# Cross-attention and feed-forward kernel: first loads on two queues, fewer warm-up matmuls, wq centred head by head on two engines

## The chip, the cores and the metric

The kernel runs on one core of a Trainium2 chip (trn2). The metric is the device time in microseconds of one execution. The kernel before took 117.61 us, the median of three runs (117.22, 117.66 and 117.61).

## The reference

```python
def xattn(x, context, Wq, Wk, Wv, Wo, bo):      # 8 heads of 128
    q = (x @ Wq).reshape(B, Tq, h, C) * SCALE    # SCALE = 128 ** -0.25
    k = (context @ Wk).reshape(B, Tk, h, C) * SCALE
    v = (context @ Wv).reshape(B, Tk, h, C)
    attn = softmax(einsum('bqhc,bkhc->bhqk', q, k))
    out = einsum('bhqk,bkhc->bqhc', attn, v).reshape(B, Tq, h * C)
    return out @ Wo + bo

x = x + xattn(layernorm(x), ctx_768, Wq, Wk, Wv, Wo, bo)
x = x + ffn(layernorm(x), Ws1, Ws2, W1, W2, Wr)
```

x is 2 x 1024 x 256, the context 2 x 77 x 192, all in fp32. The ffn is a shared expert, square(relu(x @ Ws1)) @ Ws2, and eight routed ones. Each routed one is multiplied by a truncated softmax weight of the two best logits, which is zero unless the gap between them is large. The kernel computes the largest gap and branches to the routed part only if it needs it.

## The kernel before

The kernel folds the weights first. For each head, A = (centred Wq) x (scaled K) turns the scores into x times A, so that q is never formed; in the same way U = V x Wo turns the output into probabilities times U. The mean over the 256 inputs of each column of Wq is taken off (the centring), which stands in for the mean in layernorm. A and U are split into a high and a low fp32r part (`a_hi`, `a_lo`), and so is x transposed (`xt_hi`, `xt_lo`), so that each product is three fp32r matmuls (the helper `three`, L433 to L437). After this opening come 16 tiles of 128 rows of x, each with scores, softmax, attention and feed-forward. They are software-pipelined over tiles, in a loop of two tiles a turn.

The order of work on each engine is written out by hand, with one block for each engine and semaphores between them. The part that this document is about is the opening:

- SyncE issues all the loads on its own DMA queue: ctx, the two main parts of wk, the second part of ctx, the tail of wk, four pieces of wq_t (two heads each), then x transposed, x, ws1 and wr, wv, wo, bo, ws2 and the rest of x (L336 to L364).
- TensorE runs WARM_UP = 9 matmuls on a constant (L566), each of which the trace shows as two records. Then it computes K from ctx and wk: `context_main` (L405, 8 matmuls, 16 records) and `context_tails` (L415), which need the two parts of ctx and all of wk. Then `make_a` (L429), two matmuls a head, in the order of the heads. Then the scores of tile 0, first half (`alo_ready` at least 4), a small matmul for the mean of the ffn weights (L580), the second half of the scores (all 8 of `a_lo`), and the scores of tile 1.
- VectorE sums each head of wq as it lands and scales the sum to minus the mean (`mean_of_wq`, L1074 and L1076): head 0, head 1, then three pairs. Each of the ten steps adds one to `wqs`. Then it makes the eight `a_lo` (`lo_of_a`, L1081), the centred ffn weights (L1091), and the statistics of x.
- ScalarE copies and scales K out of PSUM, two heads at a time (L741, `kt_copied`), centres heads 0, 4 and 5 (`centre_wq`, L737), and makes the eight `a_hi` (L749). Its exponentials of tile 0 follow.
- GpSimd centres heads 1, 2 and 3, 6 and 7 (L862), then splits x transposed of tiles 0 and 1 (`turned_x`, L817 and L822).

The first four banks of A are the ones that K is computed in, so `make_a` also waits for `kt_copied` of h + 1 for its first four heads, which counts pairs. The centring waits read so:

```python
if h in (0, 4, 5):
    pe.wait_ge(wqact_ready, (1, 2, 3)[(0, 4, 5).index(h)])
else:
    pe.wait_ge(wqpool_ready, {1: 1, 2: 2, 3: 2, 6: 3, 7: 3}[h])
if h < H // 2:
    pe.wait_ge(kt_copied, h + 1)
```

Of the kernel before, what the change touches and what calls it, by code (L numbers as in the profile page):

```python
# [34 lines left out]
P = 128  # L35
# [8 lines left out]
def program(nc, x, x_t, ctx_p, wq_t, wk_p, wv_p, wo, bo, ws1, ws2, w1, w2, wr, out):  # L44
    B, TQ, D = x.shape
# [15 lines left out]
    assert B == 2 and FE == P and TILES % 4 == 0 and HALF <= 512 and KC == 5 and DCH == 2  # L61
    GATE_STEPS = 5
    OPEN_FROM = 272.0
    WARM_UP = 9
    HALFP = P // 2
    assert WB == HG + 2 and HG == 4
    PB = (KC - 1) * P
# [5 lines left out]
    with ExitStack() as ctx:  # L73
# [243 lines left out]
        def wait_apart(eng, semaphore, count):  # L317
# [2 lines left out]
            eng.wait_ge(const_ready, 4)  # L320
            eng.wait_ge(semaphore, count)

        block = ctx.enter_context(nc.Block())


        @block.sync
        def _(sp):
            wq_rows = wq_t.rearrange("(h p) d -> p h d", p=P)

            def load_wq(i):  # L330
                sp.dma_start(wqt_sb[:, 2 * i:2 * i + 2, :], wq_rows[:, 2 * i:2 * i + 2, :]).then_inc(wq_in[i], 16)

            def load_wv(i):
                sp.dma_start(wv_sb[:, i, :, :].rearrange("p e c -> p (e c)"), wv_p[:, i, :]).then_inc(wv_in[i], 16)

            sp.dma_start(ctx_sb[:, 0, :], ctx_p[:, 0, :]).then_inc(ctx_in, 16)  # L336
            for i in range(2):
                sp.dma_start(wk_sb[:, i, 0:HG, :].rearrange("p e c -> p (e c)"), wk_p[:, i, 0:HG * P]).then_inc(wk_in[i], 16)
            sp.dma_start(ctx_sb[:, 1, :], ctx_p[:, 1, :]).then_inc(ctx_tail_in, 16)
            sp.dma_start(wk_sb[:, :, HG:WB, :].rearrange("p i e c -> p i (e c)"), wk_p[:, :, HG * P:WB * P]).then_inc(wk_tail_in, 16)  # L340
            for i in range(4):
                load_wq(i)

            def load_x_t(i):
                for c in range(DCH):
# [53 lines left out]
        def _(pe):  # L399
# [19 lines left out]

            def make_a():  # L420
                for h in range(H):
                    if h in (0, 4, 5):
                        pe.wait_ge(wqact_ready, (1, 2, 3)[(0, 4, 5).index(h)])
                    else:
                        pe.wait_ge(wqpool_ready, {1: 1, 2: 2, 3: 2, 6: 3, 7: 3}[h])
                    if h < H // 2:
                        pe.wait_ge(kt_copied, h + 1)
                    for c in range(DCH):
                        mm = pe.matmul(a_banks[h][:, c * BK:(c + 1) * BK], wqt_sb[:, h, c * P:(c + 1) * P],  # L429
                                       kt_sb[:, h, :], start=True, stop=True)  # L430
                    mm.then_inc(a_ready, 1)
# [246 lines left out]
        def _(act):  # L678
# [56 lines left out]
            def centre_wq(h, count):  # L735
                act.wait_ge(wqs, count)
                act.activation(wqt_sb[:, h, :], wqt_sb[:, h, :], ACT.Identity, bias=wq_mean[:, 1, h:h + 1]).then_inc(wqact_ready, 1)  # L737

            for g in range(H // 2):
                act.wait_ge(kt_ready, g + 1)  # L740
                act.activation(kt_sb[:, 2 * g:2 * g + 2, :].rearrange("p h n -> p (h n)"), s_ps[:, g, 0:2 * BK],  # L741
                               ACT.Copy, scale=SCALE2).then_inc(kt_copied, 1)
                if g == 0:
                    centre_wq(0, 2)
            centre_wq(4, 8)
            centre_wq(5, 8)
            for h in range(H):
                act.wait_ge(a_ready, h + 1)
                act.activation(a_hi[:, :, :, h * TK:(h + 1) * TK],  # L749
                               a_banks[h][:, 0:DCH * BK].rearrange("p (c b k) -> p c b k", c=DCH, b=B),  # L750
                               ACT.Copy).then_inc(ahi_ready, 1)
            exps(0, 0, 0)
            exps(0, 0, 1)
            for g in range(H // 2):
# [52 lines left out]
        def _(pool):  # L807
# [38 lines left out]
            def step(t, par):  # L846
                normalise(t, par, 0)
                if live(t + 2, TILES):
# [7 lines left out]
            pool.wait_ge(const_ready, 3)  # L856
            pool.affine_select(out=ident[:, :], in_=ident[:, :], compare_op=ALU.not_equal, fill=1.0, base=0,
                               pattern=[[-1, P]], channel_multiplier=1).then_inc(const_ready, 1)
            for first, heads, count in ((1, 1, 4), (2, 2, 6), (6, 2, 10)):
                hs = slice(first, first + heads)  # L860
                pool.wait_ge(wqs, count)
                pool.tensor_tensor(wqt_sb[:, hs, :], wqt_sb[:, hs, :],  # L862
                                   wq_mean[:, 1, hs].unsqueeze(2).broadcast_to([P, heads, D]), ALU.add).then_inc(wqpool_ready, 1)
            turned_x(0, 0)
            turned_x(1, 1)
            rstd_first(0)
# [45 lines left out]
        def _(dve):  # L912
# [141 lines left out]
            def all_stats_x(t, par):  # L1054
                stats_x(t, par)
                dve.wait_ge(bn1_done, t + 1)
                aggregate_x(t, par)
                variance_x(t, par)
# [19 lines left out]
            def lo_of_a(h):  # L1078
                dve.wait_ge(ahi_ready, h + 1)
                at = (slice(None), slice(None), slice(None), slice(h * TK, (h + 1) * TK))  # L1080
                dve.tensor_tensor(a_lo[at], a_banks[h][:, 0:DCH * BK].rearrange("p (c b k) -> p c b k", c=DCH, b=B),  # L1081
                                  a_hi[at].bitcast(F32), ALU.subtract).then_inc(alo_ready, 1)
# [4 lines left out]
                mean_of_wq(i, 2 * i, 2, 2 * i + 3)  # L1087
            for h in range(H):
                lo_of_a(h)
            dve.wait_ge(wmean_ready, 1)  # L1090
            dve.tensor_tensor(wsr_c[:, :, :], wsr_sb[:, :, :],  # L1091
                              wmean_bank[:, 0:NL].unsqueeze(1).broadcast_to([P, DCH, NL]), ALU.subtract).then_inc(wsr_ready, 1)
            dve.wait_ge(x_in[0], 32)
            all_stats_x(0, 0)
            maxima(0, 0)
            neg_maxima(0, 0)
            all_stats_x(1, 1)
# [163 lines left out]
```

## Time and profile before

| | us |
|---|---|
| runs | 117.22, 117.66, 117.61 |
| profiled execution, its own time | 117.36 |
| its span, first to last instruction | 115.5 |
| TensorE matmul busy | 109.2 (95%) |
| VectorE busy | 87.8 (76%) |
| ScalarE busy | 85.5 (74%) |
| GpSimd busy | 65.5 (57%) |

Mean granted clock of TensorE is 0.993 of full speed. The span is cut into stretches by the windows view; the chain view follows the work that ended last back from the last instruction; the timeline gives each group of instructions with its start and duration. PE is TensorE, DVE VectorE, ACT ScalarE, POOL GpSimd, SPq and ACTq the DMA-issuing queues of SyncE and ScalarE. L737 is line 737 of the kernel.

### The profile page before, as it was taken

How to read it: one execution, taken by the hardware profiler on the slowest of the kernel's cores; microseconds unless marked ns; L12 is line 12 of the kernel's file. 1: busy time of each engine (PE TensorE's matmuls, PEld its weight loads, DVE VectorE, ACT ScalarE, POOL GpSimd, SP SyncE). 2: the span in 40 equal slices, each digit the busy share in tenths (PEclk: the TensorE clock that was granted, in tenths of full speed). 3: DMA queues.
4: the chain of work that ended last, by engine and by line, in shares of the span. 5: the costliest groups of instructions: out<-in, count | busy, mean ns of one | idle time of the engine just before them, and what ended most of it. 6: DMA issues, size and time to landing. Idle time of an engine off the chain costs nothing.

```text
span 115.5 us, 3118 instructions
## 1 busy us (share of the span) xinstructions
PE 109.2 (95%) x854; PEld 105.9 (92%) x854; DVE 87.8 (76%) x350; ACT 85.5 (74%) x348; POOL 65.5 (57%) x106
## 2 busy tenths in 40 slices
PE   6976999999999999999999999999999999989981
PEld 6974999899998989999999999999999999979970
DVE  1009888569889697797979797797979696798963
ACT  4006925997948979898988889898988889994320
POOL 2005735855372965785676578657746865469250
PEclk9999999999999999999999999999999999999997
DMA  3799999994000200040005001300500050031032
GB/s 63 252 336 357 354 355 350 346 349 160 6 6 0 91 0 3 6 146 35 0 0 182 0 0 61 121 0 0 182 0 0 0 182 3 0 124 57 38 136 98
DMA packets 11815, 12.70 MB, mean 110 GB/s; under 512 B 1056, under 2 KB 10272, under 8 KB 11808
## 3 DMA queue, kind: packets, MB, share of 16 engines
q1 hardware_dynamic: 11520, 12.36, 32.4%
q10 hardware_dynamic: 288, 0.26, 0.7%
q8 instruction: 3, 0.05, 0.2%
q14 instruction: 4, 0.03, 0.1%
HBM read 8.42 MB, written 2.10 MB: 91 GB/s over the span
## 4 chain that ended last, share of the span: by engine, by line
PE 80%; DVE 7%; DMA 4%; ACT 2%; SPq 2%; issue 2%; POOL 1%; DVEq 0%; ACTq 0%
PE o_ps L435 8%; PE o_ps L437 8%; PE o_ps L436 8%; PE s_ps L435 7%; PE s_ps L437 7%; PE s_ps L436 7%; PE g_ps L493 6%; PE f_ps L523 4%; DMA wqt_sb<-in_wq_t 4%; PE g_ps L506 3%; PE f_ps L435 2%; PE g_ps L449 2%; ACT probs L712 1%; PE f_ps L437 1%; PE f_ps L436 1%
## 5 line engine op out<-in xcount | busy, mean ns | idle before, releaser
L712 ACT ACTIVATE probs<-s_ps,neg_max,rstd 128x77 f32<-128x77 f32 x112 | 45.2, 425 | 4.0 <-DVE neg_max L950 4.0
L840 POOL TENSOR_TENSOR probs<-probs,recip 128x308 f32<-128x308 f32 x27 | 18.9, 701 | 23.4 <-DVE recip L956 23.3
L712 ACT ACTIVATION_READ_ACCUMULATOR probs<-s_ps,neg_max,rstd 128x1 f32 x112 | 24.0, 214 | 0.0
L435 PE MATMUL o_ps<-u_hi,pt_hi 128*128 128x256 f32 (+1 forms) x80 | 22.7, 284 | 0.5 <-DVE pt_lo L964 0.5
L437 PE MATMUL o_ps<-u_lo,pt_hi 128*128 128x256 f32 (+1 forms) x80 | 22.4, 280 | 0.0
L436 PE MATMUL o_ps<-u_hi,pt_lo 128*128 128x256 f32 (+1 forms) x80 | 22.4, 280 | 0.0
L435 PE MATMUL s_ps<-a_hi,xt_hi 128*128 128x308 f32 x64 | 22.1, 345 | 0.0
L437 PE MATMUL s_ps<-a_lo,xt_hi 128*128 128x308 f32 x64 | 19.5, 304 | 0.0
L436 PE MATMUL s_ps<-a_hi,xt_lo 128*128 128x308 f32 x64 | 19.4, 303 | 0.0
L435 PEld LDWEIGHTS o_ps<-u_hi,pt_hi 128*128 128x128 f32 (+1 forms) x80 | 15.0, 188 | 0.9 <-DVE pt_lo L964 0.9
L436 PEld LDWEIGHTS o_ps<-u_hi,pt_lo 128*128 128x128 f32 (+1 forms) x80 | 15.1, 188 | 0.0
L437 PEld LDWEIGHTS o_ps<-u_lo,pt_hi 128*128 128x128 f32 (+1 forms) x80 | 15.0, 188 | 0.0
L942 DVE TENSOR_REDUCE row_max<-s_ps 128x8 f32<-128x616 f32 x16 | 12.4, 775 | 2.1 <-PE s_ps L437 2.1
L983 DVE TENSOR_TENSOR x_tr<-o_ps,xb_sb 128x256 f32<-128x256 f32 x14 | 5.9, 424 | 9.7 <-PE o_ps L437 9.7
L822 POOL TENSOR_TENSOR xt_lo<-xt_sb,xt_hi 128x256 fp32r<-128x256 f32 x16 | 11.7, 728 | 2.2 <-POOL xt_hi L820 0.2
L435 PEld LDWEIGHTS s_ps<-a_hi,xt_hi 128*128 128x128 f32 x64 | 12.1, 188 | 0.2 <-issue 0.2
L436 PEld LDWEIGHTS s_ps<-a_hi,xt_lo 128*128 128x128 f32 x64 | 12.1, 190 | 0.0
L437 PEld LDWEIGHTS s_ps<-a_lo,xt_hi 128*128 128x128 f32 x64 | 12.0, 188 | 0.0
L844 POOL TENSOR_TENSOR xb_sb<-x_sb,bo_sb 128x256 f32<-128x256 f32 x16 | 11.7, 737 | 0.0
L493 PE MATMUL g_ps<-ident,probs 128*128 128x128 f32 x66 | 10.1, 273 | 0.0
L968 DVE TENSOR_TENSOR pt_lo<-g_ps,pt_hi 128x512 fp32r<-128x512 f32 x13 | 8.9, 687 | 1.1 <-ACT pt_hi L698 0.6
L698 ACT ACTIVATE pt_hi<-g_ps 128x512 fp32r<-128x512 f32 x13 | 7.8, 601 | 1.7 <-PE g_ps L493 1.7
(188 smaller groups left out, 270.6 us busy)
## 6 DMA issues: line engine op xcount, KB each, us to landing
xt_sb<-in_x_t SPq DMA_DIRECT2D x8, 256.0 KB, 6.4
x_sb<-in_x SPq DMA_DIRECT2D x8, 256.0 KB, 6.3
x_sb<-x_tr SPq DMA_DIRECT2D x7, 256.0 KB, 2.3
out<-y_sb SPq DMA_DIRECT2D x6, 256.0 KB, 2.3
wqt_sb<-in_wq_t SPq DMA_DIRECT2D x4, 256.0 KB, 5.2
wo_sb<-in_wo SPq DMA_DIRECT2D x1, 1024.0 KB, 8.9
wk_sb<-in_wk_p SPq DMA_DIRECT2D x3, 256.0 KB, 3.2
wv_sb<-in_wv_p SPq DMA_DIRECT2D x2, 384.0 KB, 6.2
```

The lines of the kernel that those rows point to most:

```text
L435: pe.matmul(out_ap, hi, rhs_hi, start=first, stop=False)
L436: pe.matmul(out_ap, lo, rhs_hi, start=False, stop=False)
L437: return pe.matmul(out_ap, hi, rhs_lo, start=False, stop=last)
L493: mm = pe.transpose(to, probs_of(t)[:, par, c * P:(c + 1) * P], ident[:, :])
L698: act.activation(pt_hi[:, 0:PB], main_turned(t), ACT.Copy).then_inc(pthi_ready, 1)
L712: e = act.activation(probs_of(t)[:, par, h * TK:(h + 1) * TK], s_ps[:, 2 * par + half, (h - half * H // 2) * TK:(h - half * H // 2 + 1) * TK],
L822: pool.tensor_tensor(xt_lo[:, par, :, :], src, xt_hi[:, par, :, :].bitcast(F32), ALU.subtract).then_inc(xt_ready, 1)
L840: pool.tensor_tensor(rows, rows, recip[:, par, hs].unsqueeze(2).broadcast_to([P, H // 2, TK]), ALU.mult).then_inc(probs_ready, 1)
L844: pool.tensor_tensor(xb_sb[:, par, :], x_sb[:, t, :], bo_sb[:, :], ALU.add).then_inc(xb_ready, 1)
L942: dve.tensor_reduce(row_max[:, par, :].rearrange("p (i h) -> p i h", i=2), s_ps[:, 2 * par:2 * par + 2, 0:HALF].rearrange("p i (h k) -> p ...
L968: dve.tensor_tensor(pt_lo[:, 0:PB], main_turned(t), pt_hi[:, 0:PB].bitcast(F32), ALU.subtract).then_inc(ptlo_ready, 1)
L983: dve.tensor_tensor(x1_of(t, par), o_ps[:, 0:D], xb_sb[:, par, :], ALU.add).then_inc(x1_ready, 1)
```

## The change

WARM_UP goes from 9 to 6. Of the first nine loads, ScalarE now issues ctx part 0, wk main 1, ctx part 1, wq pieces 0 and 2, ahead of all its other work; SyncE issues wk main 0, the wk tail, wq pieces 1 and 3, and then goes on as before. ScalarE centres heads 0, 2, 4 and 6, GpSimd heads 1, 3, 5 and 7, each head by itself, and ScalarE's copies of K, centrings and `a_hi` are interleaved in a new order. VectorE takes the statistics of x of tile 0 before the centred ffn weights instead of after them.

```diff
--- before.py
+++ after.py
@@ -61,7 +61,7 @@
     assert B == 2 and FE == P and TILES % 4 == 0 and HALF <= 512 and KC == 5 and DCH == 2
     GATE_STEPS = 5
     OPEN_FROM = 272.0
-    WARM_UP = 9
+    WARM_UP = 6
     HALFP = P // 2
     assert WB == HG + 2 and HG == 4
     PB = (KC - 1) * P
@@ -320,26 +320,26 @@
             eng.wait_ge(const_ready, 4)
             eng.wait_ge(semaphore, count)
 
+        wq_rows = wq_t.rearrange("(h p) d -> p h d", p=P)
+
+        def load_wk(eng, i):
+            eng.dma_start(wk_sb[:, i, 0:HG, :].rearrange("p e c -> p (e c)"), wk_p[:, i, 0:HG * P]).then_inc(wk_in[i], 16)
+
+        def load_wq(eng, i):
+            eng.dma_start(wqt_sb[:, 2 * i:2 * i + 2, :], wq_rows[:, 2 * i:2 * i + 2, :]).then_inc(wq_in[i], 16)
+
         block = ctx.enter_context(nc.Block())
 
 
         @block.sync
         def _(sp):
-            wq_rows = wq_t.rearrange("(h p) d -> p h d", p=P)
-
-            def load_wq(i):
-                sp.dma_start(wqt_sb[:, 2 * i:2 * i + 2, :], wq_rows[:, 2 * i:2 * i + 2, :]).then_inc(wq_in[i], 16)
-
             def load_wv(i):
                 sp.dma_start(wv_sb[:, i, :, :].rearrange("p e c -> p (e c)"), wv_p[:, i, :]).then_inc(wv_in[i], 16)
 
-            sp.dma_start(ctx_sb[:, 0, :], ctx_p[:, 0, :]).then_inc(ctx_in, 16)
-            for i in range(2):
-                sp.dma_start(wk_sb[:, i, 0:HG, :].rearrange("p e c -> p (e c)"), wk_p[:, i, 0:HG * P]).then_inc(wk_in[i], 16)
-            sp.dma_start(ctx_sb[:, 1, :], ctx_p[:, 1, :]).then_inc(ctx_tail_in, 16)
+            load_wk(sp, 0)
             sp.dma_start(wk_sb[:, :, HG:WB, :].rearrange("p i e c -> p i (e c)"), wk_p[:, :, HG * P:WB * P]).then_inc(wk_tail_in, 16)
-            for i in range(4):
-                load_wq(i)
+            load_wq(sp, 1)
+            load_wq(sp, 3)
 
             def load_x_t(i):
                 for c in range(DCH):
@@ -419,10 +419,10 @@
 
             def make_a():
                 for h in range(H):
-                    if h in (0, 4, 5):
-                        pe.wait_ge(wqact_ready, (1, 2, 3)[(0, 4, 5).index(h)])
+                    if h % 2 == 0:
+                        pe.wait_ge(wqact_ready, h // 2 + 1)
                     else:
-                        pe.wait_ge(wqpool_ready, {1: 1, 2: 2, 3: 2, 6: 3, 7: 3}[h])
+                        pe.wait_ge(wqpool_ready, h // 2 + 1)
                     if h < H // 2:
                         pe.wait_ge(kt_copied, h + 1)
                     for c in range(DCH):
@@ -736,19 +736,35 @@
                 act.wait_ge(wqs, count)
                 act.activation(wqt_sb[:, h, :], wqt_sb[:, h, :], ACT.Identity, bias=wq_mean[:, 1, h:h + 1]).then_inc(wqact_ready, 1)
 
-            for g in range(H // 2):
+            act.dma_start(ctx_sb[:, 0, :], ctx_p[:, 0, :]).then_inc(ctx_in, 16)
+            load_wk(act, 1)
+            act.dma_start(ctx_sb[:, 1, :], ctx_p[:, 1, :]).then_inc(ctx_tail_in, 16)
+            load_wq(act, 0)
+            load_wq(act, 2)
+
+            def kt_pair(g):
                 act.wait_ge(kt_ready, g + 1)
                 act.activation(kt_sb[:, 2 * g:2 * g + 2, :].rearrange("p h n -> p (h n)"), s_ps[:, g, 0:2 * BK],
                                ACT.Copy, scale=SCALE2).then_inc(kt_copied, 1)
-                if g == 0:
-                    centre_wq(0, 2)
-            centre_wq(4, 8)
-            centre_wq(5, 8)
-            for h in range(H):
+
+            def hi_of_a(h):
                 act.wait_ge(a_ready, h + 1)
                 act.activation(a_hi[:, :, :, h * TK:(h + 1) * TK],
                                a_banks[h][:, 0:DCH * BK].rearrange("p (c b k) -> p c b k", c=DCH, b=B),
                                ACT.Copy).then_inc(ahi_ready, 1)
+
+            kt_pair(0)
+            centre_wq(0, 2)
+            kt_pair(1)
+            centre_wq(2, 6)
+            kt_pair(2)
+            kt_pair(3)
+            centre_wq(4, 8)
+            hi_of_a(0)
+            hi_of_a(1)
+            centre_wq(6, 10)
+            for h in range(2, H):
+                hi_of_a(h)
             exps(0, 0, 0)
             exps(0, 0, 1)
             for g in range(H // 2):
@@ -856,11 +872,10 @@
             pool.wait_ge(const_ready, 3)
             pool.affine_select(out=ident[:, :], in_=ident[:, :], compare_op=ALU.not_equal, fill=1.0, base=0,
                                pattern=[[-1, P]], channel_multiplier=1).then_inc(const_ready, 1)
-            for first, heads, count in ((1, 1, 4), (2, 2, 6), (6, 2, 10)):
-                hs = slice(first, first + heads)
+            for h, count in ((1, 4), (3, 6), (5, 8), (7, 10)):
                 pool.wait_ge(wqs, count)
-                pool.tensor_tensor(wqt_sb[:, hs, :], wqt_sb[:, hs, :],
-                                   wq_mean[:, 1, hs].unsqueeze(2).broadcast_to([P, heads, D]), ALU.add).then_inc(wqpool_ready, 1)
+                pool.tensor_tensor(wqt_sb[:, h:h + 1, :], wqt_sb[:, h:h + 1, :],
+                                   wq_mean[:, 1, h:h + 1].unsqueeze(2).broadcast_to([P, 1, D]), ALU.add).then_inc(wqpool_ready, 1)
             turned_x(0, 0)
             turned_x(1, 1)
             rstd_first(0)
@@ -1087,11 +1102,11 @@
                 mean_of_wq(i, 2 * i, 2, 2 * i + 3)
             for h in range(H):
                 lo_of_a(h)
+            dve.wait_ge(x_in[0], 32)
+            all_stats_x(0, 0)
             dve.wait_ge(wmean_ready, 1)
             dve.tensor_tensor(wsr_c[:, :, :], wsr_sb[:, :, :],
                               wmean_bank[:, 0:NL].unsqueeze(1).broadcast_to([P, DCH, NL]), ALU.subtract).then_inc(wsr_ready, 1)
-            dve.wait_ge(x_in[0], 32)
-            all_stats_x(0, 0)
             maxima(0, 0)
             neg_maxima(0, 0)
             all_stats_x(1, 1)
```

SyncE, from its first load to its last piece of wq. Before:

```order
L336 DMA ctx_sb<-in_ctx_p 128x154
L338 DMA wk_sb<-in_wk_p 128x512 x2
L339 DMA ctx_sb<-in_ctx_p 128x154
L340 DMA wk_sb<-in_wk_p 128x2x256
L331 DMA wqt_sb<-in_wq_t 128x2x256 x4
L346 DMA xt_sb<-in_x_t 128x2x256 x2
```

and with the change:

```order
L326 DMA wk_sb<-in_wk_p 128x512
L340 DMA wk_sb<-in_wk_p 128x2x256
L329 DMA wqt_sb<-in_wq_t 128x2x256 x2
L346 DMA xt_sb<-in_x_t 128x2x256 x2
L351 DMA x_sb<-in_x 128x2x256 x2
```

Of nine loads four are left on this queue (the ctx and half of the wk and wq pieces have gone), and `xt_sb`, x transposed, stands right behind its two pieces of wq.

ScalarE, from its first instruction to the last `a_hi` (`wqt_sb` is wq, head by head). Before:

```order
L741 ACT_TABLE_LOAD
L741 ACTIVATE kt_sb<-s_ps 128x308
L737 ACTIVATE wqt_sb<-wqt_sb,wq_mean 128x256
L741 ACTIVATE kt_sb<-s_ps 128x308 x3
L737 ACTIVATE wqt_sb<-wqt_sb,wq_mean 128x256 x2
L749 ACTIVATE a_hi<-s_ps 128x4x77 x4
L749 ACTIVATE a_hi<-g_ps 128x4x77 x2
L749 ACTIVATE a_hi<-o_ps 128x4x77
L749 ACTIVATE a_hi<-f_ps 128x4x77
```

and with the change, up to the first of the later `a_hi`:

```order
L739 DMA ctx_sb<-in_ctx_p 128x154
L326 DMA wk_sb<-in_wk_p 128x512
L741 DMA ctx_sb<-in_ctx_p 128x154
L329 DMA wqt_sb<-in_wq_t 128x2x256 x2
L747 ACT_TABLE_LOAD
L747 ACTIVATE kt_sb<-s_ps 128x308
L737 ACTIVATE wqt_sb<-wqt_sb,wq_mean 128x256
L747 ACTIVATE kt_sb<-s_ps 128x308
L737 ACTIVATE wqt_sb<-wqt_sb,wq_mean 128x256
L747 ACTIVATE kt_sb<-s_ps 128x308 x2
L737 ACTIVATE wqt_sb<-wqt_sb,wq_mean 128x256
L752 ACTIVATE a_hi<-s_ps 128x4x77 x2
```

Five DMA issues stand ahead of the load of the activation table, the third and fourth copy of K (`kt_sb`) stand behind the centring of head 2, and the centring of head 6 stands between the second `a_hi` and the third.

VectorE, from the last `a_lo` to the first row maxima and their negation. Before:

```order
L1081 TENSOR_TENSOR a_lo<-f_ps,a_hi 128x4x77
L1091 TENSOR_TENSOR wsr_c<-wsr_sb,g_ps 128x272
L914 BN_STATS bn<-x_sb 128x6
L917 BN_AGGR mv<-bn 128x2
L921 TENSOR_SCALAR var<-mv 128x1
L942 TENSOR_REDUCE row_max<-s_ps 128x8
L950 TENSOR_SCALAR neg_max<-row_max,rstd 128x8
```

and with the change:

```order
L1096 TENSOR_TENSOR a_lo<-f_ps,a_hi 128x4x77
L929 BN_STATS bn<-x_sb 128x6
L932 BN_AGGR mv<-bn 128x2
L936 TENSOR_SCALAR var<-mv 128x1
L1108 TENSOR_TENSOR wsr_c<-wsr_sb,g_ps 128x272
L957 TENSOR_REDUCE row_max<-s_ps 128x8
L965 TENSOR_SCALAR neg_max<-row_max,rstd 128x8
```

The centred ffn weights (`wsr_c`) have moved from ahead of the statistics of x to behind them.

## Rows read from the trace of the kernel before

**Rows 1.** Windows: busy per engine in us, granted clock, DMA share, GB/s.

```profile
16.20:28.20 12.00, 12.00 (x97) 11.68 (x96) 9.25 (x30) 9.32 (x44) 6.73 (x12) 1.00 1.02 321
...
41.40:101.30 59.90, 59.90 (x483) 59.84 (x484) 49.52 (x215) 53.05 (x230) 38.47 (x60) 1.00 0.12 44
```

**Rows 2.** Chain of waits: start us, us, what.

```profile
3.30 5.07 DMA wqt_sb<-in_wq_t
...
10.39 1.05 POOL wqt_sb L862
...
11.48 1.32 PE s_ps L429 x8
```

**Rows 3.** Timeline of the SyncE queue: start us, us, DMA issue, count.

```profile
0.74 0.39 SPq L336 DMA_DIRECT2D ctx_sb<-in_ctx_p  x1
...
1.19 0.88 SPq L338 DMA_DIRECT2D wk_sb<-in_wk_p  x2
...
2.59 0.67 SPq L340 DMA_DIRECT2D wk_sb<-in_wk_p  x1
...
3.30 2.12 SPq L331 DMA_DIRECT2D wqt_sb<-in_wq_t  x4
```

**Rows 4.** DMA issues, in order of issue: count, KB each, us to landing.

```profile
wk_sb<-in_wk_p SPq DMA_DIRECT2D x1, 256.0 KB, 2.9
...
wk_sb<-in_wk_p SPq DMA_DIRECT2D x1, 256.0 KB, 5.0
...
wqt_sb<-in_wq_t SPq DMA_DIRECT2D x1, 256.0 KB, 5.1
...
xt_sb<-in_x_t SPq DMA_DIRECT2D x2, 256.0 KB, 5.5
```

**Rows 5.** Windows of the first 10 us, columns as in rows 1.

```profile
0.00:3.00 3.00, 1.94 (x9) 1.94 (x10) 0.29 (x4) 1.28 (x1) 0.78 (x8) 1.00 0.37 71
3.00:4.00 1.00, 1.00 (x7) 1.00 (x6) 0.00 (x0) 0.00 (x0) 0.00 (x0) 1.00 0.95 338
4.00:6.00 2.00, 2.00 (x15) 2.00 (x15) 0.00 (x0) 0.00 (x0) 0.00 (x0) 1.00 0.73 214
6.00:7.00 1.00, 1.00 (x10) 0.95 (x8) 0.00 (x0) 0.00 (x0) 0.00 (x0) 1.00 1.02 315
7.00:10.00 3.00, 1.91 (x21) 1.53 (x20) 1.54 (x5) 1.40 (x4) 0.41 (x1) 1.00 1.07 349
```

**Rows 6.** Timeline of TensorE: start us, us, operation, count, idle before.

```profile
1.06 4.02 PE L567 MATMUL f_ps<-mean_of 128*128 128x128 f32 x18 [1.06 <-DVE probs L1068]
...
4.92 2.26 PE L405 MATMUL s_ps<-ctx_sb,wk_sb 128*128 128x154 f32 x16
...
7.77 1.32 PE L415 MATMUL s_ps<-ctx_sb,wk_sb 64*128 64x154 f32 x16 [0.59 <-DMA wk_sb<-in_wk_p]
```

**Rows 7.** Timeline of ScalarE.

```profile
0.74 1.28 ACT L741 ACT_TABLE_LOAD   x1 [0.74 <-PEq L1255]
...
8.57 0.43 ACT L741 ACTIVATE kt_sb<-s_ps 128x308 f32<-128x308 f32 x1 [6.54 <-PE s_ps L415]
...
11.49 0.91 ACT L737 ACTIVATE wqt_sb<-wqt_sb,wq_mean 128x256 f32<-128x256 f32 x2 [1.00 <-DVE wq_mean L1076]
...
12.30 1.36 ACT L749 ACTIVATE a_hi<-s_ps 128x308 fp32r<-128x308 f32 x4
```

**Rows 8.** Timeline of VectorE.

```profile
12.07 0.17 DVE L1076 TENSOR_SCALAR wq_mean<-wq_mean 128x2 f32<-128x2 f32 x1
...
12.74 1.64 DVE L1081 TENSOR_TENSOR a_lo<-s_ps,a_hi 128x308 fp32r<-128x308 f32 x4 [0.50 <-ACT a_hi L749]
...
15.45 0.47 DVE L1081 TENSOR_TENSOR a_lo<-f_ps,a_hi 128x308 fp32r<-128x308 f32 x1
```

**Rows 9.** Timeline of GpSimd.

```profile
13.30 0.40 POOL L817 CAST xt_hi<-xt_sb 128x256 fp32r<-128x256 f32 x1
...
13.78 0.73 POOL L822 TENSOR_TENSOR xt_lo<-xt_sb,xt_hi 128x256 fp32r<-128x256 f32 x1
```

## Prediction

> **What bounds the kernel now.** I read three views in this order. The windows by stage come first. From 16.2 us on TensorE has no idle microsecond in the opening (12.00 of 12.00) nor in the loop (59.90 of 59.90) [rows 1]. No term of the sum is in that part, so an early microsecond moves the end only if TensorE gets to its steady work sooner. The chain of waits says what holds it back: the first piece of wq lands at 3.30 + 5.07 = 8.37, VectorE's sums follow, GpSimd centres heads 2 and 3 until 11.44, and from 11.48 on TensorE works without a hole [rows 2]. The timelines show a second path that is nearly as late: the tail of wk lands at 7.6 (issued 2.59, 5.0 to landing) [rows 3, 4], TensorE has waited 0.59 us for it [rows 6], and ScalarE's first copy of K starts at 8.57, that is 0.80 after those matmuls [rows 7]. The stretch of VectorE's eight `a_lo` ends at 15.45 + 0.47 = 15.92 [rows 8]. TensorE's second half of the scores of tile 0 needs the last of them, so I take 15.92 as the mark against which the gain is counted.
>
> **Part 1: the loads on two queues.** SyncE issues each load in about 0.4 to 0.5 us [rows 3]. Before, the first piece of wq is its sixth, at 3.30. Now it is ScalarE's fourth. ScalarE began at 0.74 [rows 7], as SyncE did, so with three issues of SyncE's size it comes at 2.1. The load of the activation table (1.28) moves behind five issues, to about 3.2 to 4.5; ScalarE's first copy of K comes long after, so I cost it at nothing.
>
> Landing times have to be estimated. Up to and with the first wq piece, 1178 KB (1.21 MB) stand in the one queue. The windows moved 0.21 MB by 3.0, 0.55 by 4.0, 0.98 by 6.0 and 1.29 by 7.0 [rows 5], so that amount had passed at 6.7, and the piece landed at 8.37, 1.65 later. For wk's first part (0.34 MB) that moment is 3.4 and the landing 1.19 + 2.9 = 4.1, so it lagged only 0.7. Between 4 and 6 us the engines moved 214 GB/s with a share of 0.73, though work was queued; around it they moved 338 and 349. With two queues that share the engines evenly, twice ScalarE's 666 KB (1.36 MB) stand ahead. At 0.21 MB by 3.0 and then 340 GB/s it is through at 6.4. No lag gives 6.4, the lag of 1.65 gives 8.05, the lag of 0.7 gives 7.1. The issue time alone gives 2.1 + 5.07 = 7.2. I take **7.1**, near both middle values, and keep 6.4 and 8.05 as ends.
>
> **Part 2: six warm-up matmuls.** Eighteen records take 4.02 us, so 0.21 each. Sixteen of `context_main`, with more columns, take 2.26, so 0.13 a record [rows 6]. The clock column says 1.00 from the first window on [rows 5], but these spacings are those of the lower level (1.2 GHz) and then the upper (2.4 GHz), and the change falls about where the warm-up ends, after 3.7 us without a hole. Now the warm-up ends at 1.06 + 12 x 0.21 = 3.6. wk's first part, issued at 0.74, lands at 3.6 if it again takes 2.9. So I take `context_main` from 3.7: four records at the low level (0.26 each) until 4.8, twelve at 0.13, end 6.4. The wk tail, issued at 1.2, with the same 5.0 to landing, is there at 6.2. The tails start at 6.4 and ScalarE's first copy of K at 7.2, against 8.57.
>
> **Part 3: the chain through ScalarE.** Now ScalarE is the longest row of work in this stretch. Costs: a copy 0.43 and 0.35 in series, a centring 0.5 alone, an `a_hi` 0.35 in series [rows 7]. First copy 7.2 to 7.65. Head 0 (mean ready 0.65 after landing) to 8.25, second copy to 8.6. Head 2 waits for the sixth step of `wqs`, which came 2.02 after the landing (10.39 - 8.37, GpSimd's start) [rows 2]: 9.1, done 9.6. Behind it are queued the third and fourth copies of K, to 9.95 and 10.3. `make_a` of head 2 needs the third of them (`kt_copied`), a wait that was long over before, so TensorE starts head 2 at 9.95, against 11.48. Head 4 (its step came 3.12 after the landing, 11.49) 10.3 to 10.75, two `a_hi` to 11.4, head 6 (3.87 after the landing [rows 8], no wait) to 11.85, third `a_hi` to 12.25. VectorE's `a_lo` have a pace of 0.39 ((1.64 - 0.47) / 3) [rows 8], so the last six end at 12.3 + 5 x 0.39 + 0.47 = 14.7. The mark moves from 15.92 to 14.7: **-1.2 us**. GpSimd's four single centrings replace one and two pairs; heads 5 and 7 are wanted two heads after its turn, so they cost nothing. TensorE itself would be through A at 9.95 + 6 x 0.52 = 13.1; the scores' second half waits for the `a_lo` instead, which is what eats 0.3 of the 1.5 gained at head 2.
>
> What is late next: x transposed must be on chip about 1.2 before 13.1, since GpSimd splits it in 0.40 + 0.73 with a wait between [rows 9]. Before, it had landed by about 12 (issued from 5.46, 5.5 to landing and an issue more) [rows 4]. It is issued 2.5 us earlier, and even unchanged it would just do. The statistics of x ahead of the centred ffn weights fill a wait of VectorE and move no end, since TensorE wants those weights only after two more tiles of scores: 0.
>
> **Sum.** 0 - 1.2 + 0 = -1.2 us, from 117.36 of the profiled execution 116.15. The median of the runs is 0.25 above it, so 116.4.
>
> **Weighed against the Trainium skill.** Rows 5 show the engines not full between 4 and 6 us with a single queue feeding them. The Trainium skill, in DMA: Bandwidth & Descriptors, section "Issuing engines are not separate DMA queues", says that loads issued from several engines run on the same 16 DMA engines, and that only the sequencer's time to issue is saved. By it the sum would keep the 1.2 us of issue time and no more, which is 7.2 for the landing and nearly my figure. It speaks against the end at 6.4.
>
> **The rivals.** (a) The transfers take what they take. The lag of 1.65 comes back, because pieces of both queues are interleaved and the last engine decides. The landing is at 8.0 or later. Then the same chain gives head 2 at 10.05 to 10.55, kt copies 11.25, head 4 11.7, head 6 12.8, last `a_lo` 15.65: gain 0.25, **117.4**. The better order of centring alone is worth nothing, as ScalarE's new work stands ahead of the `a_hi`. For it: a lag of that size did grow in the first 8 us. Against it: the share of 0.73 between 4 and 6 us leaves room.
>
> (b) Slower: TensorE's clock. The warm-up now ends at 3.6, before the upper level was seen, and any wait for wk or ctx is a hole ahead of it. If the lower level then lasts through the context stage, `context_main` takes 16 x 0.26 until 7.9, the tails twice as long, and the first copy of K starts at 9.45. If the upper level comes only inside `make_a`, after its first two heads, the last head is done near 15.6 and the last `a_lo` at 16.5, +0.6; if A runs at the lower level throughout (8.4 us), +3.7. I price it between, at +1.5, **119.1**. It decides if the level rises after 7.8, since a first copy of K later than 8.55 costs the whole gain. For it: the rise was seen only after 3.7 us of unbroken work. Against it: the hole is 0.1 to 0.5 us by the landings. The Trainium skill, TensorE: Matmul & The Clock Gate, section "What's actually happening", says that the slow level is the resting state, that sustained activity releases it, and that the moment varies from run to run. That speaks for this rival; rows 6 agree with the first half.
>
> (c) More: the two queues fill the dip between 4 and 6 us fully. The landing at 6.4 gives head 2's centring 8.45 to 8.95, third copy 9.3, head 4 10.05, head 6 11.1, last `a_lo` 14.0: -1.9, **115.7**. Beyond that the K path (first copy at 7.2) holds it.
>
> **How the numbers follow.** My forecast with (c), that is a landing between 6.4 and 7.75, has 0.70: 0.55 for the forecast and 0.15 for (c). (a) has 0.19, (b) 0.11. A measurement of this kernel can tell about 0.5% (0.6 us) from no change. A landing before 7.75 gains more than that, so faster is 0.70, same (a) 0.19, slower (b) 0.11. The range goes from 115.4, the end of (c) with the scatter of the runs (0.3), to 117.7, which takes in (a) and no change, and leaves out (b) and a little.
>
> **What would show it.** Right: ScalarE's fourth issue at about 2.1; the first wq sum at 7.1; the first copy of K near 7.2; `make_a` of head 2 near 10, released by ScalarE's third copy; the last `a_lo` at 14.7; and the same loop afterwards, 59.9 us for the same tiles. Wrong: a first sum after 8 (a), or `context_main` records at 0.26 throughout (b). If the opening shrinks by 1.2 and the end does not, then some later load or ScalarE's exponentials have taken it, which I have not seen in the rows.

## The result, and the profile after

The change is slower: 117.83 us, median of 20 runs, against 117.10, the median of 20 runs of the kernel before; the ratio is 1.0056 (95% interval 1.0036 to 1.0076). The forecast was 116.4, with a range from 115.4 to 117.7. The profiled execution took 117.56 us with a span of 115.4, against 117.36 and 115.5.

So the span has hardly moved, and the loss has to be looked for in three places:

| | before | change |
|---|---|---|
| runs with a mean granted clock over 0.99: mean span | 115.32 (35 runs) | 115.44 (14 runs) |
| the same runs: mean of time less span | 1.84 | 2.18 |
| runs with a mean granted clock of 0.985 | 0 of 35 | 5 of 20, at 118.7 to 119.3 us |

The 35 runs are those of the kernel before in the first set of experiments. A sixth run of the change took 179.93 us with a mean clock of 0.56, which nothing here explains. The ratio leaves it out, with the three longest of the five, as the ratios of e1, e3 and g2 below leave out their long runs. The median of the 14 runs is 117.53, which is 0.43 of the loss of 0.73; the 0.34 (outside the span) and 0.12 (span) of the table account for it. The six others lift the median by the remaining 0.30.

The chain of waits of the changed kernel in the opening answers to [rows 2]:

```profile
2.15 6.26 DMA wqt_sb<-in_wq_t
...
9.55 0.60 DVE wq_mean L1089
...
10.38 0.51 ACT wqt_sb L737
10.89 0.32 ACT kt_sb L747
11.35 0.76 PE s_ps L429 x4
```

The first piece of wq is issued at 2.15 as forecast, and lands at 8.41, where it had landed at 8.37. "Landed" is here the issue time plus the time to landing. Head 2 of A starts at 11.35 instead of 11.48, released by ScalarE's third copy of K. Two windows of single DMA issues, pieces 1 and 0 of wq, answer to [rows 4]; the last column is us to landing:

```profile
wqt_sb<-in_wq_t SPq DMA_DIRECT2D x1, 256.0 KB, 6.3
wqt_sb<-in_wq_t ACTq DMA_DIRECT2D x1, 256.0 KB, 6.3
```

Both take 6.3 us, and land at nearly the same time, 8.2 and 8.4. Windows of the first 10 us (busy by engine, granted clock, DMA share, GB/s) answer to [rows 5]:

```profile
0.00:3.00 3.00, 1.94 (x9) 1.94 (x10) 0.29 (x4) 0.00 (x0) 0.79 (x8) 1.00 0.29 87
3.00:4.00 1.00, 1.00 (x6) 0.72 (x5) 0.00 (x0) 0.85 (x1) 0.00 (x0) 1.00 1.05 382
4.00:6.00 2.00, 2.00 (x8) 2.00 (x9) 0.00 (x0) 0.43 (x1) 0.00 (x0) 1.00 0.91 297
6.00:7.00 1.00, 1.00 (x8) 1.00 (x8) 0.00 (x0) 0.00 (x0) 0.00 (x0) 1.00 1.07 376
7.00:10.00 3.00, 2.06 (x23) 1.66 (x22) 1.50 (x5) 1.25 (x3) 0.36 (x1) 1.00 1.07 356
```

The dip between 4 and 6 us is mostly filled, 297 GB/s for 214, and 1.61 MB have passed by 7.0 where it was 1.29. The bytes come sooner; the piece that is waited for does not. TensorE, ScalarE and VectorE answer to [rows 6], [rows 7] and [rows 8]:

```profile
1.06 2.93 PE L567 MATMUL f_ps<-mean_of 128*128 128x128 f32 x12 [1.06 <-DVE probs L1083]
3.98 3.46 PE L405 MATMUL s_ps<-ctx_sb,wk_sb 128*128 128x154 f32 x16
7.37 1.32 PE L415 MATMUL s_ps<-ctx_sb,wk_sb 64*128 64x154 f32 x16
```

```profile
3.15 1.28 ACT L747 ACT_TABLE_LOAD   x1 [3.15 <-issue]
8.19 0.43 ACT L747 ACTIVATE kt_sb<-s_ps 128x308 f32<-128x308 f32 x1 [3.76 <-PE s_ps L415]
...
10.38 0.51 ACT L737 ACTIVATE wqt_sb<-wqt_sb,wq_mean 128x256 f32<-128x256 f32 x1 [0.49 <-DVE wq_mean L1091]
10.80 0.73 ACT L747 ACTIVATE kt_sb<-s_ps 128x308 f32<-128x308 f32 x2
```

```profile
15.23 0.48 DVE L1096 TENSOR_TENSOR a_lo<-f_ps,a_hi 128x308 fp32r<-128x308 f32 x1
```

The sixteen records of `context_main` take 3.46 us instead of 2.26, since more of them run at the lower clock level, and the first copy of K starts at 8.19. The last `a_lo` ends at 15.71, 0.2 before the mark of 15.92. TensorE is busy throughout the later stages, as in [rows 1]:

```profile
16.20:28.20 12.00, 12.00 (x97) 11.68 (x97) 8.96 (x30) 9.47 (x44) 6.96 (x12) 1.00 0.94 299
...
41.40:101.30 59.90, 59.90 (x484) 59.76 (x484) 49.54 (x214) 53.10 (x231) 38.56 (x60) 1.00 0.12 44
```

### The profile page after: what moved, and what is told of

The parts are those of the page before. It is cut to its first block, busy times and chain, and to the rows that moved or that the text cites. A ratio compares the mean times of both kernels' runs of the same rounds, so it can differ in the third digit from the quotient of the medians.

```text
span 115.4 us, 3108 instructions
## 1 busy us (share of the span) xinstructions
PE 109.4 (95%) x848; PEld 105.8 (92%) x848; DVE 87.6 (76%) x350; ACT 86.1 (75%) x349; POOL 65.4 (57%) x107
## 4 chain that ended last, share of the span: by engine, by line
PE 80%; DVE 7%; DMA 5%; ACT 3%; issue 2%; ACTq 1%; DVEq 0%
PE o_ps L435 8%; PE o_ps L437 8%; PE o_ps L436 8%; PE s_ps L435 7%; PE s_ps L436 7%; PE s_ps L437 7%; PE g_ps L493 6%; DMA wqt_sb<-in_wq_t 5%; PE f_ps L523 4%; PE g_ps L506 3%; PE f_ps L435 2%; PE g_ps L449 2%; ACT probs L712 1%; PE f_ps L437 1%; PE f_ps L436 1%
```

## Experiments

A label such as e1 names a run of a changed kernel, and the quoted text under it is what was expected before it ran. Ratios are against the kernel before, run beside each one. "Long runs" are those with a mean granted clock of 0.985. Spans and times outside the span are means over the other runs.

| | ratio (95%) | span | outside | long runs |
|---|---|---|---|---|
| e1 change, 9 warm-ups | 1.0033 (1.0004 to 1.0062) | 115.31 | 2.18 | 3 of 12 |
| e2 before, 6 warm-ups | 0.9991 (0.9969 to 1.0013) | 115.09 | 1.85 | 0 of 12 |
| e3 loads alone | 1.0033 (1.0008 to 1.0058) | 115.50 | 2.01 | 2 of 12 |
| e4 order alone | 0.9977 (0.9956 to 0.9997) | 115.10 | 1.83 | 0 of 12 |
| e5 change, wait filled | 1.0030 (1.0009 to 1.0052) | 115.44 | 2.17 | 0 of 12 |
| e6 order and 6 warm-ups | 1.0003 (0.9981 to 1.0026) | 115.24 | 1.84 | 0 of 12 |
| e8 change, wq piece 0 early | 1.0019 (0.9993 to 1.0045) | 115.10 | 2.16 | 0 of 12 |
| e9 one load on ScalarE | 0.9945 (0.9925 to 0.9966) | 114.63 | 1.81 | 0 of 12 |
| f1 e9 and the order | 0.9932 (0.9906 to 0.9958) | 114.49 | 1.83 | 0 of 9 |
| f2 both ctx on ScalarE | 0.9983 (0.9957 to 1.0009) | 115.05 | 1.83 | 0 of 12 |
| f3 f2 and the order | 0.9954 (0.9927 to 0.9982) | 114.83 | 1.82 | 0 of 12 |
| f4 wq in one queue | 0.9932 (0.9906 to 0.9959) | 114.48 | 1.80 | 0 of 12 |
| g1 f4, 6 warm-ups | 0.9881 (0.9846 to 0.9915) | 113.82 | 1.81 | 0 of 6 |
| g2 f4, wq 2 and 3 on ScalarE | 1.0036 (1.0012 to 1.0059) | 115.37 | 2.15 | 2 of 12 |
| g3 f4, wq 1 MB later | 1.0283 (1.0240 to 1.0325) | | | 6 of 6 |

### The three parts of the change, apart

e1, the change with

```diff
-    WARM_UP = 6
+    WARM_UP = 9
```

> The changed kernel with 9 warm-up matmuls instead of 6. Theory C (clock: the hole between the six warm-ups and the first context matmul, 3.6 to 4.0 us, delays the upper TensorE level or loses it again in some executions): 0.996 to 1.000 of the kernel before, and no run with a mean granted clock near 0.985 (5 of 20 runs of the change had that, with 118.7 to 119.3 us). Theory L (the loads on two queues cost): still 1.003 to 1.006. Theory O (the new order of centring and of the activations costs): still 1.003 to 1.006.

e2, the kernel before with

```diff
-    WARM_UP = 9
+    WARM_UP = 6
```

> The kernel before with 6 warm-up matmuls instead of 9 and nothing else. Theory C: 1.003 to 1.010, with some runs at a mean granted clock near 0.985 and 1 to 2 us longer; the hole is longer here than in the change, since wk's first part lands at 4.05. Theories L and O: 1.000, since wq's first piece lands at 8.4 in any case.

e3, the kernel before with the change's loads and nothing else:

```diff
+            load_wk(sp, 0)
...
-            for i in range(4):
-                load_wq(i)
+            load_wq(sp, 1)
+            load_wq(sp, 3)
...
+            act.dma_start(ctx_sb[:, 0, :], ctx_p[:, 0, :]).then_inc(ctx_in, 16)
+            load_wk(act, 1)
+            act.dma_start(ctx_sb[:, 1, :], ctx_p[:, 1, :]).then_inc(ctx_tail_in, 16)
+            load_wq(act, 0)
+            load_wq(act, 2)
```

> The kernel before with the nine first loads shared by the queues of SyncE and ScalarE as in the change, 9 warm-ups, old centring. Theory C: 0.998 to 1.001, no run at 0.985; the first piece of wq lands near 8.4 as in the change's profile, so TensorE's make_a starts at 9.6 as before. Theory L: 1.003 to 1.006.

e4, the change with 9 warm-ups and all loads on SyncE in the old order, so that this is left of it:

```diff
-            for first, heads, count in ((1, 1, 4), (2, 2, 6), (6, 2, 10)):
+            for h, count in ((1, 4), (3, 6), (5, 8), (7, 10)):
...
+            kt_pair(0)
+            centre_wq(0, 2)
+            kt_pair(1)
+            centre_wq(2, 6)
...
```

> The kernel before with the new centring and orders of ScalarE, GpSimd and VectorE, all loads on SyncE's queue, 9 warm-ups. Theory C: 0.998 to 1.000, the stretch of A 0.1 us earlier as in the change's profile (head 2 at 11.35 against 11.48). Theory O: 1.003 to 1.006.

The loads alone give most of the loss of the normal runs (mean time 117.51 in e3, against 117.16 before and 117.61 in the change), and the long runs come with them, with 9 warm-ups as with 6. Six warm-ups alone cost nothing that can be measured, so my first theory, that they leave a hole which delays the clock and costs the loss, falls. The order alone has a span 0.2 us shorter; e2 has the same span (115.09) and an interval that takes in no change, so this gain is barely above the noise. The moment at which the upper level comes differs from execution to execution, with 6 warm-ups and with 9: with 9 the sixteen records of `context_main` take from 2.26 us (before) to 3.33 (e4). In e2's profile `context_main` takes 2.48 us,

```profile
4.00 2.48 PE L405 MATMUL s_ps<-ctx_sb,wk_sb 128*128 128x154 f32 x16
```

and in that of e6 (the order of e4 with 6 warm-ups, same loads) 3.90:

```profile
3.97 3.90 PE L405 MATMUL s_ps<-ctx_sb,wk_sb 128*128 128x154 f32 x16
```

e6 against e4:

```diff
-    WARM_UP = 9
+    WARM_UP = 6
```

> The kernel before with the new centring and orders and 6 warm-ups, all loads on SyncE's queue. If the shared loads are all that costs: 0.996 to 0.998 of the kernel before (order alone measured 0.9977, six warm-ups alone 0.9991), time outside the span 1.84 us, no run near 0.985. If six warm-ups and the new order only harm each other together: 1.000 or more.

e6 came out at 1.0003, which by the number is the second case. The intervals of e2, e4 and e6 overlap, so it is not shown that six warm-ups and the order harm each other, and I leave this open.

### The long runs: TensorE's wait ahead of `make_a`

e5, the change with

```diff
+    FILL = 6
...
+            for _ in range(FILL):
+                pe.matmul(f_ps[:, 0:P], mean_of[:, :], mean_of[:, :], start=True, stop=True)
             make_a()
```

> The changed kernel with six matmuls on the constant (1.3 us at the upper level) between the context tails and make_a, where TensorE waits for the first piece of wq. Theory H (the loads let the K matmuls finish earlier but wq's first piece not, so the hole ahead of make_a grows; where a clock window falls on it, the level drops for 3.4 us and the run is 1.5 to 2 us longer): no run with a mean granted clock near 0.985 in 12 (10 of 44 runs of the three kernels with shared loads had one), the others 117.5 as in the change. Rival D (the drop comes from the transfers of two queues themselves or from chance): 2 to 4 of 12 runs near 0.985 still.

TensorE in e5's profile: the tails, the six fillers, `make_a`.

```profile
6.62 1.32 PE L416 MATMUL s_ps<-ctx_sb,wk_sb 64*128 64x154 f32 x16 [0.29 <-DMA wk_sb<-in_wk_p]
7.86 1.60 PE L577 MATMUL f_ps<-mean_of 128*128 128x128 f32 x12
10.26 1.46 PE L430 MATMUL s_ps<-kt_sb,wqt_sb 128*128 128x154 f32 x8 [0.79 <-ACT wqt_sb L740]
```

None of 12 runs was long, where the change, e1 and e3 had 10 of 44, and the 12 took what the change's normal runs take. By chance alone, at a rate of 10 in 44, that happens once in 22 times (0.773 to the power 12 is 0.045). e8 (below) helps: it has five early loads on ScalarE's queue and wq on both queues, as the change has, and none of its 12 runs was long either, which makes it 0.002 for the 24. So the drop goes with TensorE's waits rather than with two queues as such. The fillers shorten the wait and do not close it: in this execution wq's first piece landed at 9.03, and 0.79 us were left, against 0.94 in the change's profile. g3 widens the wait on purpose, from f4 (below):

```diff
-            for i in range(4):
-                load_wq(sp, i)
...
             load_x_t(0)
             load_x(0)
+            for i in range(4):
+                load_wq(sp, i)
```

> The same kernel with the four pieces of wq behind the first pieces of x transposed and x, 1 MB later. It widens the hole of TensorE between the context tails and make_a to about 3 us (tails end near 8, make_a starts near 11). Theory H: most or all runs have a mean granted clock near 0.985, and the profile shows the lower level for one stretch of 3.4 us just after the hole, while make_a and the first scores run at 0.26 a record; beside the later wq (1.5 to 3 us) that costs another 1.5 us, 119.5 to 122 us in all. Rival D: the mean clock stays over 0.99 and the run is only 1.5 to 3 us longer.

```profile
7.15 1.32 PE L415 MATMUL s_ps<-ctx_sb,wk_sb 64*128 64x154 f32 x16 [0.19 <-DMA ctx_sb<-in_ctx_p]
11.99 4.47 PE L429 MATMUL s_ps<-kt_sb,wqt_sb 128*128 128x154 f32 x16 [3.52 <-ACT wqt_sb L737]
```

The windows of the same execution (granted clock third from the end):

```profile
8.00:10.00 2.00, 0.47 (x8) 0.24 (x4) 0.00 (x0) 0.41 (x1) 0.00 (x0) 1.00 1.08 372
10.00:12.00 2.00, 0.01 (x1) 0.01 (x1) 1.14 (x5) 0.57 (x2) 0.00 (x1) 0.78 1.14 338
12.00:14.00 2.00, 2.00 (x8) 2.00 (x9) 1.93 (x5) 1.51 (x5) 1.64 (x3) 0.50 1.03 374
14.00:16.00 2.00, 2.00 (x9) 2.00 (x9) 1.19 (x5) 1.73 (x5) 1.74 (x4) 0.50 1.10 353
16.00:18.00 2.00, 2.00 (x9) 2.00 (x9) 0.90 (x3) 0.86 (x2) 1.19 (x3) 0.51 1.10 348
18.00:20.00 2.00, 2.00 (x17) 2.00 (x16) 1.57 (x4) 1.29 (x3) 0.00 (x0) 1.00 1.10 349
```

In an idle time of 3.52 us the granted clock goes from 1.00 to 0.50, that is from 2.4 to 1.2 GHz, between 10 and 12 us, and it is back near 18. The sixteen `make_a` records from 11.99 on take 4.47 us, where g1's below take 2.6 (1.32 + 1.29). All six runs had it, with mean clocks below 0.99. In this execution (mean clock 0.972, 121.83 us) the low stretch lasted twice as long as I had expected; the five others, at 0.984 to 0.986 and 119.84 to 121.15 us, had about what I expected: a mean of 0.985 over a span of 118.6 us is 3.6 us at half the clock (2 x 0.015 x 118.6), an estimate.

This shows what a wait there does. Where the long runs of the change, e1 and e3 had their drop is inferred, since no profile fell on one of them. A wait ahead of `make_a` is not all of it. g2 (below) had 2 long runs of 12, and its profile has 0.38 us there and 0.72 ahead of head 2:

```profile
9.34 1.34 PE L429 MATMUL s_ps<-kt_sb,wqt_sb 128*128 128x154 f32 x8 [0.38 <-ACT wqt_sb L737]
11.40 1.29 PE L429 MATMUL s_ps<-kt_sb,wqt_sb 128*128 128x154 f32 x8 [0.72 <-ACT kt_sb L747]
```

The kernel before has three waits in its profile, of 0.59, 0.50 and 0.43 us, and none of its 119 runs beside the experiments was long. Which wait must be how long for the drop was not found.

### Why wq does not come earlier

e8, the change with piece 0 in SyncE's queue ahead of the wk tail:

```diff
             load_wk(sp, 0)
+            load_wq(sp, 0)
             sp.dma_start(wk_sb[:, :, HG:WB, :]...
-            load_wq(sp, 1)
-            load_wq(sp, 3)
+            load_wq(sp, 2)
...
-            load_wq(act, 0)
-            load_wq(act, 2)
+            load_wq(act, 1)
+            load_wq(act, 3)
```

> The changed kernel with wq's pieces 0 and 2 on SyncE's queue, piece 0 ahead of the wk tail, and pieces 1 and 3 on ScalarE's. My sum rested on wq's first piece landing at 7.1, which it did not (8.4). If the rest of the sum holds, the piece lands at 6 to 7.2 here, make_a's head 2 starts at 10 to 10.7, the span is 0.4 to 1.0 us shorter than the change's (114.5 to 115.0), the drop near 0.985 is rarer, and the time outside the span stays 2.18: 0.997 to 1.001 of the kernel before. If the K path is the bound as well, head 2 stays at 11.3 and the ratio at 1.003.

The piece landed at 5.6, earlier than expected, and left the chain; the wk tail took its place:

```profile
1.65 6.22 DMA wk_sb<-in_wk_p
...
8.01 0.81 PE s_ps L415 x8
8.82 0.41 ACT kt_sb L747
...
9.68 2.41 PE s_ps L429 x16
```

It is issued at 1.65 and lands at 7.87. A is reached at 9.68, no earlier than in the change (9.63), but it runs on without the wait at head 2. The span fell by 0.34, a little less than I had expected, and the K path is the bound.

e9 moves the first load alone:

```diff
-            sp.dma_start(ctx_sb[:, 0, :], ctx_p[:, 0, :]).then_inc(ctx_in, 16)
...
+            act.dma_start(ctx_sb[:, 0, :], ctx_p[:, 0, :]).then_inc(ctx_in, 16)
```

> The kernel before with only the first load, ctx part 0, issued by ScalarE. It asks for the time outside the span (1.84 us before, 2.01 with the loads alone, 2.18 in the change). If any early DMA of ScalarE costs it, 2.0 to 2.2 here; if it grows with their number or with ScalarE's program, 1.84 to 1.9. The span falls by 0.2 us at most (wk's first part is issued at 0.74).

It beats every version so far. In its profile wq's first piece, issued at 2.8, landed at 7.0, and no DMA is in the chain (in e1's and e6's there was none either); TensorE's own warm-up and K matmuls are:

```profile
5.28 2.26 PE s_ps L404 x16
7.53 0.77 PE s_ps L414 x8
8.31 0.41 ACT kt_sb L741
```

I had given it 0.2 us; its span fell by 0.67. f2 moves the second part of ctx too; f1 is e9 and f3 is f2 with the centring and orders of e4:

```diff
-            sp.dma_start(ctx_sb[:, 1, :], ctx_p[:, 1, :]).then_inc(ctx_tail_in, 16)
...
+            act.dma_start(ctx_sb[:, 1, :], ctx_p[:, 1, :]).then_inc(ctx_tail_in, 16)
```

> The kernel before with both parts of ctx issued by ScalarE, 9 warm-ups, old centring. The wq pieces stay in one queue, each issued 0.9 us earlier than before. Theory Q (wq's first piece lands early only where the other pieces of wq stay behind it in its own queue): it lands at 6.6 to 7.4, span 114.5 to 114.8, ratio 0.993 to 0.996. If ScalarE's second early load already costs what five cost: 0.998 or more, outside the span 2.0.

> Only ctx part 0 on ScalarE's queue (0.9945 of the kernel before when alone) and the new centring and orders (0.9977 when alone), 9 warm-ups. If the two gains add: 0.992 to 0.994, span 114.3 us. If both only move the same bound: 0.994 to 0.996.

> Both parts of ctx issued by ScalarE and the new centring and orders, 9 warm-ups. Theory Q with gains that add: 0.991 to 0.994. Otherwise as the kernel with the loads alone.

All three are faster than before or equal. f1 came out as expected. f2 and f3 missed: their spans are 0.3 to 0.4 us longer than those of e9 and f1, the time outside the span stayed at 1.83, and wq's first piece, though issued at 2.4 instead of 2.8, landed at 7.6 in both. That landing is not in the chain of f2's profile; the K matmuls are, which took 2.92 us where e9's took 2.26:

```profile
5.27 2.92 PE s_ps L403 x16
8.19 0.77 PE s_ps L413 x8
```

These are single executions whose upper level came at different moments, so why the means differ stays open. f4 is the change with 9 warm-ups and one thing undone:

```diff
-            load_wq(sp, 1)
-            load_wq(sp, 3)
+            for i in range(4):
+                load_wq(sp, i)
...
-            load_wq(act, 0)
-            load_wq(act, 2)
```

> The changed kernel with 9 warm-ups and all four pieces of wq on SyncE's queue, behind wk's first part and tail; ScalarE issues ctx part 0, wk main 1 and ctx part 1. It undoes the part of the sharing that lets wq's pieces run side by side. Theory Q: the first piece lands at 6.8 to 7.6 instead of 8.2 to 8.4, span 114.5 to 114.9 against 115.3, no or few runs near 0.985. Rival (any early sharing costs): 115.3 as with 5 loads on ScalarE. Outside the span: 1.84 if it goes with more than three loads, 2.0 to 2.2 if three are enough.

Piece 0, issued at 1.90, takes 5.0 us to landing and is there at 6.9:

```profile
wqt_sb<-in_wq_t SPq DMA_DIRECT2D x1, 256.0 KB, 5.0
```

The span falls from 115.31 (e1) to 114.48, the long runs go, and so does the extra time outside the span. So it is the splitting of wq over two queues that loses; sharing ctx and wk gains. g1 is f4 with

```diff
-    WARM_UP = 9
+    WARM_UP = 6
```

> The kernel with wq in one queue and its other loads shared (0.9932), but with the change's 6 warm-ups. If six warm-ups are harmless once wq's first piece lands at 7: 0.991 to 0.994 and no run near 0.985. If they cost in the changed kernel by themselves: 0.995 or more, or some runs near 0.985.

It is the fastest kernel of the study, 115.57 us against 117.11, and better than either case that I had allowed. Its chain is TensorE's own work from the start:

```profile
1.08 2.91 PE f_ps L567 x12
3.99 2.44 PE s_ps L405 x16
6.43 0.77 PE s_ps L415 x8
7.20 0.41 ACT kt_sb L745
7.61 0.40 ACT wqt_sb L737
8.06 1.32 PE s_ps L429 x8
9.47 1.29 PE s_ps L429 x8
```

and the last `a_lo` ends at 13.84:

```profile
13.36 0.48 DVE L1094 TENSOR_TENSOR a_lo<-f_ps,a_hi 128x308 fp32r<-128x308 f32 x1
```

Here six warm-ups pay: the span falls by another 0.66. In f4's profile the K matmuls start at 5.17, in g1's at 3.99, and K is now what A waits for.

g2 is f4 with

```diff
-            for i in range(4):
-                load_wq(sp, i)
+            load_wq(sp, 0)
+            load_wq(sp, 1)
...
+            load_wq(act, 2)
+            load_wq(act, 3)
```

> The same kernel (9 warm-ups) with wq's pieces 2 and 3 on ScalarE's queue and 0 and 1 on SyncE's. It has five early loads on ScalarE as the change has, but in another order. Theory N (the 0.34 us outside the span goes with five early loads on ScalarE's queue, whatever they are): outside 2.0 to 2.2, span 114.4 to 114.8 as the first piece still lands near 7 to 7.8 with piece 2 beside it. Rival: outside 1.80, so it is not their number.

This is the closest test of the splitting. Piece 0 is issued at 1.90 on SyncE's queue as in f4, behind the same loads, and only has pieces 2 and 3 on the other queue; it takes 6.1 us where it took 5.0, and lands at 8.0:

```profile
wqt_sb<-in_wq_t SPq DMA_DIRECT2D x1, 256.0 KB, 6.1
```

The landing was later than I had allowed (7 to 7.8), and the span 115.37, not 114.4 to 114.8. Piece 1 (issued at 2.53) is later still, and lands at 9.49:

```profile
2.53 6.96 DMA wqt_sb<-in_wq_t
9.51 0.70 DVE wq_mean L1089
...
10.94 0.32 ACT kt_sb L747
```

The time outside the span is 2.15 again with five early loads on ScalarE's queue, and 1.80 to 1.83 with one, two or three. With the old order of ScalarE (e3) five gave 2.01, so their number is not all of it. Four were not tried, nor five small ones, so number and bytes are not told apart.

## Why the prediction was wrong

**Part 1 failed**, at the step "twice ScalarE's 666 KB stand ahead" and the landing of 7.1. The landing was 8.41, later than the worst end that I kept (8.05). At 7.0 us 1.61 MB had passed, more than the 1.36 that I had put ahead of the piece, and it was not there. The 1.36 had passed at 6.3, so the lag that I put between 0 and 1.65 was 2.1. I had counted an even share of bytes ahead of the piece and nothing for what runs beside it. The other pieces of wq had left their place behind piece 0 and ran beside it; pieces 0 and 1 landed within 0.2 us of each other. With all of wq in one queue behind the same shared loads, piece 0 takes 5.0 and 4.6 us to landing instead of 6.3, and lands at 6.9 (f4) and 6.5 (g1); with two pieces put back on the other queue it takes 6.1 (g2). The same loads can land 0.8 us apart (7.8 to 8.5 in before, e2, e4 and e6), so a single landing says little, but the four profiles with the change's loads (the change, e1, e3, e5) gave 8.2 to 9.0. The Trainium skill, DMA: Bandwidth & Descriptors, section "Queues, rings and completion order", says that each DMA engine goes round robin between the queues by packets; the landings at 8.2 and 8.4 agree. The rule of the Trainium skill that a second issuing engine saves only issue time, which I weighed, was too kind here: the 1.15 us of issue time saved were spent before the landing.

**Part 2** was right in its mechanism and mis-sized: the first copy of K starts at 8.19, not 7.2, because the upper level came later in this execution. In g1's profile it starts at 7.2. The late copy was not what A waited for in the change's profile, wq was. Two terms were too small. The six warm-ups ended at 3.99, not 3.6, and the K matmuls started at 3.98, not 3.7. And about nine of the sixteen records of `context_main` ran at the lower level instead of four (an estimate: 3.46 us at 0.26 and 0.13 a record).

**Part 3** holds. Head 2 was to start 2.85 after the landing, behind the third copy of K; it started 2.94 after it, and was released by that copy. Rival (a), the landing at 8.0 or later with a gain of 0.25 in the opening, is what the profile shows (0.2), and (a) had 0.19. That its number came so near is partly luck: its chain was summed for a landing at 8.0, and at 8.41 it would put the last `a_lo` at 16.06, after the mark. ScalarE got to its third `a_hi` about 0.3 us sooner than the chain has it. Where wq is early the chain gives what (c) said: the last `a_lo` at 14.0 by the sum, at 13.84 in g1.

**What no part had** is the 0.34 us outside the span. The profile of before has no row for it, and my sum took time less span as fixed at 1.86, without a reason. The runs show that it goes with five early loads on ScalarE's queue, and not why. The base hid part of the miss: the forecast set out from 117.61, the median of three runs, and twenty have 117.10, from which the same -1.2 would have given 115.9.

**Rival (b)** had the clock but the wrong place. I put the danger in the hole that six warm-ups leave at 3.6 us. As far as the runs show, it is in TensorE's waits for wq around `make_a`: the K matmuls are ready earlier, wq is not, and the wait between them grows. The Trainium skill, TensorE: Matmul & The Clock Gate, section "HAM oscillation — how this bites in real kernels", describes waits for DMA that bring the low level back. g3's windows, 1.00 to 0.50 in 3.52 us of idling, agree.

**In sum** the forecast of -1.2 us became -0.2 in the profiled opening, +0.34 outside the span, and 1.4 us more in 5 of the 20 runs. The chance of 0.11 for slower was too small, above all since a kernel that waits less evenly can lose through the clock without any instruction being added.

## What to carry to other kernels

Share first loads over two queues by who is waited for, not by count: move early ones of other tensors (here ctx and half of wk) and keep the pieces of one tensor that are consumed in order in one queue, or the first of them lands with the next. When one input of a matmul stage is sped up and the other is not, look at the length of TensorE's waits in that stage, and at the granted clock of many executions, not of one profile. Compare time less span as well as span when loads are given to another engine's queue.

## What the runs showed of the hardware

- With five early loads on ScalarE's queue the time outside the span is 2.15 to 2.18 us instead of 1.84 (2.01 in e3); with up to three it is 1.80 to 1.83. Where in the execution this lies was not found.
- After an idle TensorE the low level held until about 18 us in the profiled execution of g3, through 6 us of unbroken matmuls. The mean clocks of its other five runs give about half as long a low stretch.
- A 256 KB piece took 5.0 and 4.6 us to landing with the other pieces of its tensor behind it in its queue (f4, g1), and 6.1 with two of them on the other queue (g2).
- The same K matmuls took from 2.26 to 3.90 us in different executions (2.26 in the kernel before, 3.90 in e6), by when the upper level came.
